# A 2048-token Mamba, attention and MoE kernel: the parts of the Mamba scan's front change steps, and so does the add of the block before

## What is computed

```python
def _mamba_fwd(x, in_proj_w, in_proj_b, conv_w, conv_b, x_proj_w, x_proj_b, dt_proj_w, dt_proj_b, D, out_proj_w, out_proj_b):
    xc, z = jnp.split(x @ in_proj_w + in_proj_b, 2, axis=-1)       # 256 + 256
    xc = jax.nn.silu(causal_conv_of_4_taps(xc, conv_w) + conv_b)
    dBu = xc @ x_proj_w + x_proj_b
    delta_s, B, u = jnp.split(dBu, [d_state, 2 * d_state], axis=-1)  # 16 + 16 + 256
    delta = jax.nn.softplus(delta_s @ dt_proj_w + dt_proj_b)
    # for each of 16 states n:  h_n(t) = exp(-(n+1) delta(t)) h_n(t-1) + delta(t) B_n(t) u(t)
    y = sum_of_the_16_states + u * D
    y = y * jax.nn.silu(z)
    return y @ out_proj_w + out_proj_b
...
x = x + _L1_attn_ref(_layernorm(x, axis=-1), ...)
```

## Time and profile before

| | us |
|---|---|
| median of 3 executions | 1366.45 |
| lowest, highest | 1365.14, 1378.29 |
| the profiled execution | 1378.29 |
| its span, first to last instruction | 1376.6 |

### The profile page before, as it was taken

One profiled execution on the slowest core, in us unless ns is written; L12 is line 12 of the kernel. 1 busy time (PEld: TensorE's weight loads), 2 busy tenths in 40 slices (PEclk: granted clock), 3 DMA queues, 4 the chain that ended last, 5 costly groups with the idle time before them and its releaser, 6 DMA issues.

```text
span 1376.6 us, 15993 instructions
## 1 busy us (share of the span) xinstructions
PE 1197.3 (87%) x5776; PEld 603.1 (44%) x5776; DVE 904.7 (66%) x1684; ACT 782.9 (57%) x1135; POOL 291.6 (21%) x208
## 2 busy tenths in 40 slices
PE   4669886788999999999999999999968879779998
PEld 2345453343433333333333365655533334237776
DVE  4566866688788788887863264344467978984443
ACT  3667752354544565555678844545768677525554
POOL 3223344210000000000000110100056968750000
PEclk9779878899999999999999999999989899899999
DMA  2222157524300000000000121221131312200000
GB/s 91 62 62 63 47 100 114 102 31 90 43 1 1 1 1 1 2 1 1 1 2 24 58 72 32 91 64 36 40 107 63 116 69 108 88 12 0 8 8 16
DMA packets 52111, 62.98 MB, mean 46 GB/s; under 512 B 7864, under 2 KB 42304, under 8 KB 49984
## 3 DMA queue, kind: packets, MB, share of 16 engines
q1 hardware_dynamic: 52032, 61.95, 17.3%
HBM read 51.05 MB, written 4.46 MB: 40 GB/s over the span
## 4 chain that ended last, share of the span: by engine, by line
PE 54%; DVE 18%; ACT 10%; POOL 6%; issue 4%; DMA 1%; SPq 1%; DVEq 0%; POOLq 0%; ACTq 0%
DVE mx L1142 9%; PE psum L1230 8%; PE psum L1513 7%; PE psum L1200 6%; PE psum L1130 6%; PE psum L388 5%; PE psum L390 5%; PE psum L389 5%; PE psum L1905 4%; POOL drive L1954 3%; ACT probs L1214 2%; DVE hst L1972 1%; ACT psum L1914 1%; DMA kz<-qk_part_rows 1%; PE psum L1203 1%
## 5 line engine op out<-in xcount | busy, mean ns | idle before, releaser
L1214 ACT ACTIVATE probs<-psum 128x1024 f32<-128x1024 f32 (+1 forms) x320 | 288.4, 938 | 207.2 <-PE psum L1200 106.5
L1142 DVE TENSOR_REDUCE mx<-psum 128x1 f32<-128x512 f32 (+3 forms) x640 | 345.6, 602 | 67.0 <-PE psum L1130 50.4
L1130 PE MATMUL psum<-kz,qa 128*128 128x512 bf16 (+3 forms) x640 | 194.2, 356 | 39.3 <-DVE mx L1142 22.9
L1200 PE MATMUL psum<-qa,kz 128*128 128x512 bf16 (+1 forms) x640 | 186.0, 365 | 5.1 <-ACT probs L1214 2.8
L1905 PE MATMUL psum<-hst,ident 128*128 128x512 f32 x256 | 133.7, 669 | 34.7 <-DVE hst L1972 18.0
L1954 POOL TENSOR_TENSOR drive<-du,b_bc 128x1024 f32<-128x1024 f32 x64 | 149.3, 2354 | 11.7 <-DVE hst L1972 11.0
L1230 PE MATMUL psum<-probs,v 128*32 128x512 f32 (+3 forms) x1280 | 150.6, 543 | 0.1
L1531 DVE TENSOR_TENSOR hid<-hid,gate_bc 128x1024 f32<-128x1024 f32 x64 | 78.8, 1242 | 109.0 <-ACT hid L1523 106.9
L1523 ACT ACTIVATE hid<-psum,cols 128x512 f32<-128x512 f32 x128 | 85.0, 689 | 76.2 <-PE psum L390 75.7
L1972 DVE TENSOR_TENSOR_SCAN hst<-psum,hlast,drive 128x512 f32<-128x512 f32 x96 | 115.5, 1262 | 15.6 <-ACT psum L1914 10.0
L1130 PEld LDWEIGHTS psum<-kz,qa 128*128 128x128 bf16 x640 | 61.2, 99 | 142.0 <-DVE mx L1142 85.3
(11 more groups left out here) (293 smaller groups left out, 1844.0 us busy)
## 6 DMA issues: line engine op xcount, KB each, us to landing
b_bc<-b_rows SPq DMA_DIRECT2D x16, 1024.0 KB, 4.7
cs_bc<-cs_rows SPq DMA_DIRECT2D x16, 512.0 KB, 6.2
gate_bc<-gate_rows SPq DMA_DIRECT2D x32, 256.0 KB, 3.2
ew_raw<-experts_dram SPq DMA_DIRECT2D x8, 512.0 KB, 3.5
qk_part_rows<-qk_parts SPq DMA_DIRECT2D x8, 384.0 KB, 2.7
qa<-qk_part_rows SPq DMA_DIRECT2D x48, 64.0 KB
kz<-qk_part_rows SPq DMA_DIRECT2D x96, 32.0 KB
fw_raw<-net_dram SPq DMA_DIRECT2D x11, 256.0 KB, 2.7
```

What stands on the lines that cost most here:

```text
L1130: ins = pe.matmul(out[:, 0:w], qa[:, b, h // 2, i * P:(i + 1) * P], kz[:, h // 8, c, h % 8, 0:w], start=True, stop=not last, skip_group_ch ...
L1142: dve.tensor_reduce(mx[:, 4 * i + h % 4, c:c + 1], fill_bank("mx", k, n)[:, 0:w], AX.X, ALU.max).then_inc(S["mx_read"], 1)
L1200: ins = pe.matmul(out[:, lo:], kz[:, h // 8, kt // TPB, h % 8, kt % TPB * P:(kt % TPB + 1) * P], qa[:, b, h // 2, lo:], start=True, stop=n ...
L1214: act.activation(probs[:, st % 2, hh, :, lo:], s_pair[n % 2][:, :, lo:], ACT.Exp, scale=SCALE).then_inc(S["p_done"], 1)
```

## The change

It moves parts of the front in the tables of PE, ACT and the ring, the add and the bias of the block before, and one of three weight splits. It also replaces the explicit number on which ACT's ln waits by the last number that ACT has given.

- dt from step 9 to 8, z from 11 to 9, u from 13 to 11 on PE and from 13 to 12 on ACT, ln from 12 to 11; abs stays at 10, and now comes behind z.
- DVE's add (`POST_DVE`) from step 6 to 8, POOL's bias (`POST_POOL`) from 8 to 9. PE's output projection stays at 7.
- The third weight chunk from step 14 to 13 on ACT (and SP), from 15 to 14 on POOL.

```diff
-        FRONT_PE = [(0, "turn"), (1, "x"), (7, "db"), (9, "dt"), (11, "z"), (13, "u")]
-        FRONT_ACT = [(-1, "apply"), (0, "hi"), (2, "x"), (2, "tap"), (6, "xc"), (7, "db"), (9, "dt"), (10, "abs"),
-                     (11, "z"), (12, "ln"), (13, "u")]
+        FRONT_PE = [(0, "turn"), (1, "x"), (7, "db"), (8, "dt"), (9, "z"), (11, "u")]
+        FRONT_ACT = [(-1, "apply"), (0, "hi"), (2, "x"), (2, "tap"), (6, "xc"), (7, "db"), (8, "dt"), (9, "z"),
+                     (10, "abs"), (11, "ln"), (12, "u")]
         FRONT_DVE = [(-3, "stats"), (3, "conv0"), (4, "conv1"), (12, "delta"), (13, "du")]
         FRONT_POOL = [(-3, "ln")]
-        RING_FRONT = [(0, "turn"), (1, "x"), (2, "tap"), (7, "db"), (9, "dt"), (11, "z"), (13, "u")]
+        RING_FRONT = [(0, "turn"), (1, "x"), (2, "tap"), (7, "db"), (8, "dt"), (9, "z"), (11, "u")]
         EARLIEST = -3
-        POST_Y, POST_PE, POST_DVE, POST_POOL = 3, 7, 6, 8
-        FW_ACT, FW_POOL = {3: 0, 4: 1, 14: 2}, {4: 0, 5: 1, 15: 2}
+        POST_Y, POST_PE, POST_DVE, POST_POOL = 3, 7, 8, 9
+        FW_ACT, FW_POOL = {3: 0, 4: 1, 13: 2}, {4: 0, 5: 1, 14: 2}
...
                 act.wait_ge(S["c_dt_read"], 2 * b + 2)
                 o.did(act.activation(da1[:, :, :], dv1[:, :, :], ACT.Abs))
                 o.wait()
-                abs_done[b] = o.did(act.activation(da1[:, :, :], da1[:, :, :], ACT.Exp, scale=-1.0))
+                o.did(act.activation(da1[:, :, :], da1[:, :, :], ACT.Exp, scale=-1.0))
             else:
-                act.wait_ge(S["act_order"], abs_done[b])
+                o.wait()
                 act.activation(da1[:, :, :], da1[:, :, :], ACT.Ln, bias=one[:, 0:1]).then_inc(S["dt_lnd"], 1)
 
         conv1_at = {}
-        abs_done = {}
```

## The result

The changed kernel takes 1385.39 us in the median of 6 executions (1379.85 to 1390.69), beside 1366.11 us (1365.14 to 1378.29, 6 executions) for the kernel before. The ratio is 1.012 with a 95% interval of 1.0089 to 1.0153, so it is 12 to 21 us slower. The profiled execution has a span of 1387.2 us.

A forecast was written before the change was run, and what follows sets the result against it. No engine fills the scan stage; DVE's scans wait for ACT's decays. Blocks 0 to 3 (+1.8, +5.3, +4.6, -0.6) and PE's clock (+3.2) sum to +14.3 us on the 1366.45 median: 1380.8 us, range 1369.5 to 1387.

The follow-up runs named there:

- add at 8 alone: The kernel before with only DVE's add at step 8 and POOL's bias at 9; ratio 1.001 (0.9986 to 1.0035).
- z beside xc: The kernel before with z directly behind xc at step 6 on PE and ACT, both Silu; ratio 0.9971 (0.9947 to 0.9994).

## What to carry to other kernels

When instructions are moved in an order written by hand, list for every shared buffer who frees it and where the freeing instruction stands in its own engine's order: here two moves that cost 4.4 and 1.4 us alone cost 17 together, because one asked sooner and the other freed later. Moving a heavy step earlier gained nothing by itself here, where its engine had no lead to spend; what gained was to put two steps with the same activation table next to each other, and a light step kept between the heavy ones took the loss of the early z away. Compare such kernels over a stretch between two instructions that all of them have, since here the code ahead of it moved single profiles by up to 13 us.

## What was unexpected of the hardware

- An idle gap of PE costs more than its length, and not the same each time: two gaps of 3.23 us in one execution left the granted clock at 0.50 for 3.5 us and 0.56 for 3.0 more in the one case, and at 0.65 for 2.8 us in the other. The two cost 3.1 and 1.8 us from scan 8 on. Three matmuls of no use in the gap kept the clock at full pace. Behind a gap that no edit touched the clock differed too: db in block 0 took 1.93 to 1.96 us in some profiles and 3.15 to 3.18 in others. The Trainium skill (TensorE: Matmul & The Clock Gate, "Why this matters for your kernels") advises against such gaps; the trace agrees.
- A load of the activation table that belongs to a waiting instruction came behind the wait here: 2.14 us of waiting and then 1.28 of loading for z in the changed kernel. In the kernel's code the wait stands ahead of the activation; whether the load can be put ahead of it no run here shows.
- VectorE's delta (two inputs in SBUF) takes 3.39 us beside POOL's drive that began 0.04 us sooner (3.40 with the add at 8 alone) and 1.20 to 1.25 everywhere else in the twelve profiles. Who comes first decides: in block 2 of "z beside xc" the drive began 0.16 us behind delta, and delta took 1.25 us and the drive 3.32 instead of 2.36; the weight split that began 0.56 us into delta in the changed kernel took 1.76 instead of 1.27. In both orders the second one takes about as much longer as the first one still had to run. The Trainium skill (GPSIMD Engine Reference, "1. Specifications") names this contention; the trace agrees.
